# The first stage of an attention and expert-layer kernel, moved beside the attention steps

## What is computed

```
x = x + xattn(layernorm(x), ctx, ctx)
x = x + ffn(layernorm(x), weights of 8 experts)

# xattn: 32 query heads of width 32, in 8 groups of 4 that share a key head
scores  = einsum('bkgsd,bktd->bkgst', q, k) / sqrt(32)
weights = softmax(scores, axis=-1)
out     = einsum('bkgst,bktd->bkgsd', weights, v)      # v = k = ctx

# ffn: every token picks the expert with the largest gate
score  = sum over 8 columns of (select_weight . normalised x_diff)^2
gate   = sigmoid(slope * (score - center))
result = (1 - gate.max) * x + gate.max * (bias + degen . (update . (x - debias)))
```

## Time and profile before

| what | value |
|---|---|
| median of 3 runs | 1289.37 us |
| the profiled execution | 1287.5 us |
| its span, first to last instruction | 1285.5 us |
| busy in the span: PE / DVE / ACT / POOL | 79% / 74% / 53% / 60% |
| stage one, to the first matmul of stage two | 166.4 us |
| stage two, from there to the first sum of stage three | 869.2 us |
| stage three, the rest of the span | 249.9 us |

### The profile page before, as it was taken

How to read it: one execution, slowest core, us unless ns; L and a number is a source line. 1 busy time by engine, 2 the same in 40 slices (tenths; PEclk the granted TensorE clock), 3 DMA queues, 4 the chain that set the end, 5 groups by cost and what they waited for, 6 DMA issues and landing times. The chain is left out here.

```text
span 1285.5 us, 18606 instructions
## 1 busy us (share of the span) xinstructions
PE 1021.0 (79%) x6442; PEld 373.2 (29%) x6442; DVE 945.9 (74%) x1074; ACT 682.0 (53%) x1237; POOL 766.5 (60%) x341
## 2 busy tenths in 40 slices
PE   4555229999999999899999998999997737777776
PEld 3444201222222222122222221222221136556553
DVE  7888367888878888788888887888888138655554
ACT  2323106676767676667676766676765423323320
POOL 2111006787877787778787877787877674333330
PEclk9999999999999999999999999999999968988889
DMA  9999611242432333424323334243232380556543
GB/s 276 298 310 307 196 46 38 67 106 58 108 87 75 88 83 82 101 61 106 90 74 90 82 82 106 57 108 88 74 89 64 129 294 34 201 211 222 211 170 131
DMA packets 197816, 163.80 MB, mean 127 GB/s; under 512 B 56412, under 2 KB 181340, under 8 KB 197732
## 3 DMA queue, kind: packets, MB, share of 16 engines
q1 hardware_dynamic: 197732, 162.70, 43.1%
HBM read 107.84 MB, written 54.53 MB: 126 GB/s over the span
## 5 line engine op out<-in xcount | busy, mean ns | idle before, releaser
L538 ACT ACTIVATE probs<-st_ps 128x512 f32<-128x512 f32 x1024 | 554.2, 595 | 275.5 <-PE st_ps L443 270.0
L575 DVE TENSOR_REDUCE row_max<-s_ps 128x4 f32<-128x2048 f32 x256 | 584.6, 2284 | 111.6 <-PE s_ps L421 111.6
L358 POOL TENSOR_TENSOR sums<-probs 128x2048 f32<-128x2048 f32 x64 | 290.4, 4537 | 142.3 <-ACT probs L538 142.3
L365 POOL TENSOR_TENSOR sums<-probs 128x2048 f32<-128x2048 f32 x64 | 291.2, 4549 | 65.1 <-ACT probs L538 65.1
L443 PE MATMUL st_ps<-q_stack,k_stack 97*128 97x512 f16 x1024 | 320.2, 387 | 6.0 <-ACT probs L538 1.6
L453 PE MATMUL o_ps<-probs,v_in 128*32 128x512 f32 x2048 | 274.5, 608 | 6.5 <-issue 6.0
L421 PE MATMUL s_ps<-k_high,q_high 32*128 32x512 f16 x1024 | 103.4, 394 | 100.2 <-DVE row_max L575 54.2
L443 PEld LDWEIGHTS st_ps<-q_stack,k_stack 97*128 97x128 f16 x1024 | 67.4, 97 | 302.4 <-ACT probs L538 166.1
L465 PE MATMUL st_ps<-sums,ones 128*32 128x512 f32 x1024 | 123.1, 599 | 3.5 <-issue 3.5
L690 POOL TENSOR_TENSOR xa<-xa,at 128x1024 f32<-128x1024 f32 x32 | 75.0, 2354 | 84.2 <-DMA at<-attended 76.8
L281 PE MATMUL q_ps<-ident,xn 128*128 128x128 f32 x256 | 62.9, 427 | 64.4 <-DVE xn L238 64.4
(11 more groups left out here) (87 smaller groups left out, 661.5 us busy)
## 6 DMA issues: line engine op xcount, KB each, us to landing
q_stack<-q_split SPq DMA_DIRECT2D x192, 128.0 KB, 2.5
xin<-in_x_dram SPq DMA_DIRECT2D x32, 512.0 KB, 4.3
q_split<-q_parts SPq DMA_DIRECT2D x16, 1024.0 KB, 5.7
attended<-o_all SPq DMA_DIRECT2D x64, 256.0 KB, 4.3
xa<-in_x_dram SPq DMA_DIRECT2D x32, 512.0 KB, 7.8
at<-attended SPq DMA_DIRECT2D x32, 512.0 KB, 9.0
out_dram<-x_out SPq DMA_DIRECT2D x32, 512.0 KB, 2.8
q_high<-q_split SPq DMA_DIRECT2D x64, 128.0 KB, 2.2
```

The costliest lines, as they stand in the source:

```text
L358: pool.tensor_tensor(sums[:, (u - 1) % 2, 1], probs[:, (u - 1) % 2, 2], probs[:, (u - 1) % 2, 3], ALU.add).then_inc(back_done, 1)
L365: pool.tensor_tensor(sums[:, u % 2, 0], probs[:, u % 2, 0], probs[:, u % 2, 1], ALU.add).then_inc(front_done, 1)
L538: act.activation(probs[:, s, t, g, :], st_ps[:, bank_of(place(n)), :], ACT.Exp, scale=EXP_SCALE).then_inc(exped, 1)
L575: dve.reduce_max(row_max[:, u % 2, t:G * ST:ST], s_ps[:], AX.X).then_inc(reduced, 1)
```

## The change

Stage one is no longer a stage. Its work is done inside stage two's block:

- Tiles 0 to 3 (the first batch) go through ahead of the attention steps, and tile 4 up to its split. Tiles 5 to 31 are worked off one in two steps: `tile_of(u) = (u + 2) // 2 + 5`, so for u from -2 to 51. In an even step DVE takes the statistics of the tile (t = 1, 2, 3), and PE and ACT do the three transposed pieces of the tile before (t = 0, 1, 2). In an odd step POOL takes the inverse root (ahead of its first sum), DVE centres (t = 0), makes the low part of the context (t = 1) and of the tile (t = 2), and ACT makes the high parts (t = 0, 1, 2).
- The split into high and low float16 parts is made in token order, from SBUF to SBUF, ahead of the transposes. PE then transposes float16 blocks: 20 for a tile (16 of 128x128 from `q_tok`, 4 from `k_tok`) instead of 10 of float32, in three pieces. Each piece takes one bank of the rotation `st_ps`, and ACT copies it out (128x1024, 128x1024 and 128x512 elements).
- The order in which banks are filled, and which use of a bank comes before which, is now a written-out list (`filled`, `bank_before`).
- Buffers: the input tiles live in `xa0`. `at0` is gone as a kept buffer; the first four tiles of the attention output are loaded at the start of stage three. `sums` has three slots instead of four, so POOL's back sum of unit u-1 waits for the denominators of unit u-2 (`den_done`, one unit later than before).
- SP loads one tile each even step, stores two tiles each fourth step, and waits for the stored parts of a batch before it loads that batch's first unit.

```
-                pe.wait_ge(consts_set, 3)
...
-                        for h in range(KV):
-                            pe.transpose(q_ps[:, k, h, :], xn[:, k, h * P:(h + 1) * P], ident[:])
...
+            filled = [("part", n, i) for n in range(ST) for i in range(PIECES)]
+            for u in range(-AHEAD, UNITS + 2):
...
+                    if u % 2 == 0 and t < PIECES and ST <= tile_of(u) - 1 < TILES:
+                        filled.append(("part", tile_of(u) - 1, t))
+            bank_of = {use: i % BANKS for i, use in enumerate(filled)}
+            bank_before = {use: filled[i - BANKS] for i, use in enumerate(filled) if i >= BANKS}
...
-                for u in range(UNITS + 2):
+                for u in range(-AHEAD, UNITS + 2):
+                    if u % 2 == 1 and whole(tile_of(u)):
+                        inverse_root(tile_of(u))
                     if live(u - 1):
                         wait(pool, exped, NSC * u)
-                        wait(pool, den_done, u - 2)
...
+                        wait(pool, den_done, u - 1)
...
+                        if (u + 3) % KV == 0:
+                            sp.wait_ge(split_out, 64 * ((u + 3) // KV + 1))
                         load_unit(sp, u + 3)
+                    if u % 2 == 0 and n + 1 < TILES:
+                        load_x(n + 1)
...
+                    bank = st_ps[:, bank_of["part", n, i], :].bitcast(f16)
+                    for part in range(2):
+                        for c in range(chunks):
+                            last = pe.transpose(bank[:, (part * chunks + c) * P:(part * chunks + c + 1) * P],
+                                                src[:, part, (first + c) * P:(first + c + 1) * P], ident16[:])
...
+                    act.activation(dst, st_ps[:, bank_of["part", n, i], :].bitcast(f16)[:, 0:2 * chunks * P]
+                                   .rearrange("p (l c s) -> p l c s", l=2, c=chunks), ACT.Copy
+                                   ).then_inc(part_taken, 1)
...
+                def centre(n):
+
+                    dve.wait_ge(rstd_done, n + 1)
+                    wait(dve, q_low_done, n)
+                    dve.tensor_scalar(xn, xin[:, n % 2, :], mv[:, 0:1], rstd[:],
+                                      ALU.subtract, ALU.mult).then_inc(xn_done, 1)
...
+                def low_q(n):
+
+                    dve.wait_ge(q_high_done, 2 * (n + 1))
+                    dve.scalar_tensor_tensor(out=q_tok[:, 1, :], in0=xn, scalar=UP, in1=q_tok[:, 0, :],
+                                             op0=ALU.mult, op1=ALU.subtract).then_inc(q_low_done, 1)
...
+                        if t == 0 and late:
+                            centre(n)
                         if t == 1 and live(u - 2):
                             invert(u - 2)
+                        if t == 1 and early:
+                            moments(n)
+                        if t == 1 and late:
+                            low_k(n)
+                        if t == 2 and early:
+                            variance(n)
+                        if t == 2 and late:
+                            low_q(n)
...
-            at = [at0, sb("at1", [P, ST, E], f32)]
+            at = [sb(f"at{i}", [P, ST, E], f32) for i in range(2)]
...
+                for t in range(ST):
+                    sp.dma_start(at[0][:, t, :], a_tiles[t]).then_inc(t_in[t], 16)
```

More of the change, by code:

```diff
@@ L110, in xattn_ffn @@
[L110 to L114, removed]
+            BANKS, SUMS = 3, 3
+            row_max = sb("row_max", [P, 2, G * ST], f32)
+            shift = sb("shift", [G * ST, 2, P], f16)
+            v_in = sb("v_in", [P, 2, ST, D], f32)
+            probs = sb("probs", [P, 2, ST, G, S], f32)
@@ L288, in _ @@
-            @block.scalar
-            def _(act):
-                def body(b, last):
-                    for t in range(ST):
-                        n, k, pair, half = ST * b + t, t % 2, t // 2, t % 2
-                        cols = slice(half * P, (half + 1) * P)
-                        act.wait_ge(turned, n + 1)
-                        if half == 0:
-                            wait(act, split_out[pair], 32 * b)
-                        act.activation(q_parts[:, pair, 0, :, cols], q_ps[:, k], ACT.Copy, scale=UP
-                                       ).then_inc(high_done, 1)
-                        act.activation(k_parts[:, pair, 0, :, cols], k_ps[:, k, 0:CB], ACT.Copy, scale=UP
-                                       ).then_inc(high_done, 1)
-                batches(act, body)
@@ L364, in _ @@
                         wait(pool, den_done, u - 1)
[L365 removed]
+                        pool.tensor_tensor(sums[:, 2 * u % SUMS], probs[:, u % 2, 0], probs[:, u % 2, 1],
                                            ALU.add).then_inc(front_done, 1)
@@ L464, in denominators @@
                         for g in range(G):
-                            last = pe.matmul(st_ps[g * D:(g + 1) * D, bank_of(DEN_PLACE), :], ones[:, 0:D],
-                                             sums[:, u % 2, part, g, :], start=(part == 0), stop=(part == 1))
+                            last = pe.matmul(st_ps[g * D:(g + 1) * D, bank_of["den", u, 0], :], ones[:, 0:D],
+                                             sums[:, (2 * u + part) % SUMS, g, :], start=(part == 0), stop=(part == 1))
                     last.then_inc(den_done, 1)
@@ L541, in _ @@
                             make_shift(u + 1)
+                        if u % 2 == 0 and t < PIECES and ST <= tile - 1 < TILES:
+                            take_part(tile - 1, t)
                 ffn_weights()
```

371 lines of the change are left out of this document (181 added, 190 removed).

## The result

The changed kernel took 1334.97 us (median of four runs, 1333.04 to 1337.9) against 1288.18 for the kernel before: a ratio of 1.0367, 95% interval 1.0334 to 1.0401. It is slower by 47 us. The forecast was 1384, slower by 95: right in direction, and the change twice too large.

The account below looks back on a forecast made before the run. A loop between engines, not one full engine, was taken to bound stage two at 12.58 us a step. 1287.5 - 122 + 4 + 208 + 1 + 4 = 1382.5 profiled, plus 1.9 for the median: about 1384 us, range 1318 to 1450.

Parts of the forecast that it names:

- What goes away: Ahead of stage two: first row scores at 44.5 instead of 166.4 us, -122 us.
- The two steps of DVE work ahead of unit 0: Two steps before unit 0, where DVE alone is the pace: tile 5 adds +4 us.
- The port: Odd steps: POOL's sums and DVE's centring and low part block each other; centring then starts at 5.15, low part at 14.4.
- A pair is 14.6 + 18.5 = 33.1 against 25.16: +8.0, times 26 = +208: Stage two, u = 0 to 51: an even plus an odd step grows by 8.0 us, over 26 pairs +208 us.
- The reference: Stage two before the change: a step is 12.58 us, a pair 25.16, read between first reductions of two steps.
- The odd step: Stage two, step with centring and low part on DVE: 18.5 us, both waiting for POOL's sums.
- The even step: Stage two, step with statistics and transposed pieces: 12.58 + 2.0 = 14.6 us.
- The tail: Start of stage three: four loads of `at` are issued only there, +4 us (+2 to +8).
- Rival of PE's clock: Stage two: PE idles, its clock falls and it falls behind too, +2 to +5 us a pair, 1435 to 1510 us; 13%.
- only one of the two collides: Odd steps: only centring or only the low part is held by POOL, pair 30.5 to 31.0, 1317 to 1330 us; 15%.
- the case that did occur: The change as costed, both instructions held by POOL's sums: 62%, own range 1355 to 1425 us.

Follow-up runs that it names:

- the memsets: The changed kernel with POOL's two sums of each step replaced by a memset of the same output; 1210.96 us, ratio 0.9383.
- the version in idle slots: The changed kernel with centring moved to t = 3 of the even step and the low part to t = 3 of the odd step; 1217.77 us, ratio 0.9426.
- the kernel with both edits: The changed kernel with centring cut into 1023 and 1 columns and the low part moved to t = 3 of the odd step; 1329.08 us, ratio 1.0242.

## Why the prediction was wrong, point by point

- **What goes away.** Right as a sum, and in part by luck: -121.2 measured, -122 worked out, first row scores at 45.24 instead of 44.5. The last copies of tile 3 ended at 35.5, not 32.3, since the copies of tile 2 waited for the store of the first two tiles, a wait that the prediction doesn't have:

```profile
26.89 1.94 ACT L471 ACTIVATE q_parts<-st_ps 128x1024 f16<-128x1024 f16 x2 [5.30 <-DMA k_split<-k_parts]
```

  From there the last stores and the first loads took 9.8 us instead of the 12 worked out, which made up for most of it. The two steps of DVE work ahead of unit 0 cost +1.1, not +4, since part of it stood in the 0.72 us that DVE had waited for PE there.
- **The port.** Right in kind: POOL's sums hold both instructions, shown by their ends, by the memsets and by the version in idle slots. That the cause is a shared port is argued and not measured here.
- **The failed step is "A pair is 14.6 + 18.5 = 33.1 against 25.16: +8.0, times 26 = +208".** The mechanism was right and its size too large: measured 14.24 + 17.68 = 31.92 against 25.65, +6.28 a pair, +163.2 us. The excess of 45 us is nearly all of the 48 by which the forecast was too high. It has three parts, and 1.6 us from rounding 7.94 to 8.0:
  - *The reference* (12.6 us of the excess). One step of 12.58 stood for all. The mean pair before was 666.8 / 26 = 25.65. The row with the wait for `k_high` was to be had in the view of waits before the prediction; I read one step's timeline and didn't compare it with the length of the stretch.
  - *The odd step* (21 us), 18.5 worked out, 17.68 on average. After POOL's end a held instruction needed 0.56 and 1.08 us, not its full 0.81 and 1.18; what of it was done while it waited isn't shown. POOL's back sum also started 0.40 after the reduction instead of 0.6, and its normalisation started behind the inversion and didn't wait for the context's low part. Together the front sum came 0.9 earlier in the step.
  - *The even step* (9 us), 14.6 worked out, 14.24 on average. In the step shown, the statistics cost +0.74 at t = 1 instead of +1.1, since consecutive DVE instructions overlap by some 0.1 us; the piece +0.94 at t = 0 instead of +0.8, with 0.61 us for 8 float16 transposes and 0.45 of waiting for an exponential.
- **The tail.** +5.0 with step 52, worked out as +5. Stage three gave 1.3 back.
- **Rival of PE's clock.** It was held likely in one case of eight as something that adds to the time. The lower clock did come in every odd step looked at and added little: it lay behind DVE's wait. Only the two long steps of the changed kernel, 18.95 and 19.22 instead of 17.6, have it in their length, some 3 us in all. It became 0.92 us a pair when the wait for the low part was taken away.
- **The range.** It held the measured time (1335 in 1318 to 1450), but by luck: its lower end was set for the case "only one of the two collides", which did not occur (1317 to 1330 was its time, and both collisions are in the trace). The range given to the case that did occur, 1355 to 1425, didn't hold it.

The gain at the start wasn't lost: 121 us came in full. Steps 0 to 51 took 163 us more, and 120 of these came from the place of two instructions in DVE's order. With them moved, the work of stage one still costs 43 us in these steps, and 72 us of the gain are kept.

## What to carry to other kernels

Before an instruction of DVE is put beside another engine's work, ask not how long it is but what POOL is doing at that place of the step; a `tensor_scalar` from SBUF to SBUF or an instruction with two SBUF inputs ends, as the runs here have it, a fixed 0.55 or 1.08 us after POOL's sum. Put it where POOL waits: the low part then cost nothing, since it lay beside work of PE, and centring 0.5 to 0.6 us a pair of steps. Multiply by the mean of all steps, taken from the length of the stretch, and not by the one that was read in the timeline.

## What the runs showed of the hardware that was not expected

- A column count of 1023 instead of 1024 doesn't free a `tensor_scalar` from the hold (2.73 us against 2.75 on average).
- A memset of POOL holds a `tensor_scalar` from SBUF to SBUF (2.43 us instead of 0.81) and doesn't hold an instruction with two SBUF inputs (1.22 us, started 0.37 before the memset's end).
- A held instruction finishes sooner after the hold than it would take alone, and always by the same: 0.55 us instead of 0.77 for centring, 1.08 instead of 1.22 for the low part. The hold shows in the duration and not as idle time.
- With PE busy 0.39 us in three, the granted clock was at the lower level in the next three (0.50 to 0.55), and in some steps stayed there for 9 us of full work (636 to 645). Whether it did so differed between steps that were otherwise alike; there were eight of them among 26 in the profile of the kernel with both edits, whose runs spread from 1310 to 1330 us. What decides it isn't shown.
